# y times t1 in 128x128 tiles, and another order of PE's last products, in an NCHW convolution sequence on one core

## The reference

```python
t1 = p1_w * x                                   # p1_w (1, 128, 64, 1)
t2 = x + t1
t7 = einsum('oc,nchw->nohw', p7_w, relu(x))
t8 = unfold(t7, 1, 5, dilation (1, 3), pad (0, 6))
t9 = x[:, :, None] - t8
t5 = unfold(x, 3, 7, pad (1, 3))                # 21 taps of each channel
t10 = einsum('ngihw,goi->ngohw', t2 in 4 groups, p10_w)
t11 = einsum('nck,nmk->ncm', t1, t5) / sqrt(h * w)
t12 = t9.mean(2)                                # over the 5 taps
t13 = einsum('ncm,nmk->nck', t11, t10) / sqrt(c * 21)
out = maximum(t13, t12)
```

## Time and profile before

| | |
|---|---|
| median of 3 runs | 408.89 us (408.26 to 410.04) |
| profiled execution | 409.05 us, span 407.1 us |
| PE busy | 395.0 us, 97% |
| DVE busy | 333.5 us, 82% |
| ACT busy | 249.5 us, 61% |
| POOL busy | 89.2 us, 22% |
| instructions | 12373, of them PE 5126 matmuls and 5126 loads |
| granted TensorE clock | 1.00 |

### The profile page before, as it was taken

One profiled execution on the slowest core, in us unless ns is written; L12 is line 12 of the kernel. 1 busy time (PEld: TensorE's weight loads), 2 busy tenths in 40 slices (PEclk: granted clock), 3 DMA queues, 4 the chain that ended last, 5 costly groups with the idle time before them and its releaser, 6 DMA issues.

```text
span 407.1 us, 12373 instructions
## 1 busy us (share of the span) xinstructions
PE 395.0 (97%) x5126; PEld 253.8 (62%) x5126; DVE 333.5 (82%) x401; ACT 249.5 (61%) x714; POOL 89.2 (22%) x75
## 2 busy tenths in 40 slices
PE   7999999999999999999999999999999999999985
PEld 2333756668666686666888886444766668444673
DVE  7999958999688887888888887888868889686814
ACT  1336628776677745777277770777727776477980
POOL 0672201232033200332003320033201330033200
PEclk9999999999999999999999999999999999999999
DMA  8973362563766347663575634745455443643105
GB/s 314 405 292 111 105 219 62 183 215 114 293 190 218 112 156 225 197 225 97 174 239 204 190 128 153 255 167 164 163 208 181 162 160 100 208 130 104 53 30 208
DMA packets 24104, 72.40 MB, mean 178 GB/s; under 512 B 2800, under 2 KB 3056, under 8 KB 24048
## 3 DMA queue, kind: packets, MB, share of 16 engines
q1 hardware_dynamic: 24048, 71.61, 51.7%
HBM read 54.82 MB, written 16.78 MB: 176 GB/s over the span
## 4 chain that ended last, share of the span: by engine, by line
PE 85%; issue 5%; POOL 3%; DVE 2%; DMA 1%; ACT 1%; SPq 0%; DVEq 0%; ACTq 0%; POOLq 0%
PE ps_y L681 45%; PE ps_y L693 16%; PE ps_p L693 12%; PE ps_t L693 12%; POOL t1T L219 3%; DMA xw<-x_conv 1%; ACT t L314 0%; DVE v_planes L490 0%; DVE ps_y L509 0%; DVE ps_y L512 0%; DVE v_planes L467 0%; ACT base L259 0%; DVE base L565 0%; DVEq L43 0%; SPq L142 0%
## 5 line engine op out<-in xcount | busy, mean ns | idle before, releaser
L681 PE MATMUL ps_y<-v_planes,u_planes 64*64 64x512 f32 x2048 | 257.9, 590 | 1.1 <-DVE v_planes L469 0.7
L681 PEld LDWEIGHTS ps_y<-v_planes,u_planes 64*64 64x64 f32 x2048 | 127.8, 133 | 91.9 <-issue 42.2
L219 POOL TENSOR_TENSOR t1T<-t1T,p1T_sb 128x512 f32<-128x512 f32 x64 | 83.3, 1329 | 281.1 <-DVE box L540 153.2
L314 ACT ACTIVATE t<-xn,p_plus 128x64 f32<-128x64 f32 x512 | 128.2, 335 | 0.0
L693 PE MATMUL ps_p<-box,p_fifth 64*64 64x512 f32 x464 | 124.7, 590 | 0.7 <-issue 0.7
L693 PE MATMUL ps_t<-t,aT 64*64 64x512 f32 x448 | 119.7, 590 | 0.0
L259 ACT ACTIVATE base<-ps_p 128x512 f32<-128x512 f32 x58 | 34.6, 597 | 84.6 <-PE ps_p L693 84.6
L693 PEld LDWEIGHTS ps_y<-t1T,yT 64*64 64x64 f32 x2048 | 58.8, 133 | 8.0 <-DVE yT L522 3.7
L693 PE MATMUL ps_y<-t1T,yT 64*64 64x128 f32 x2048 | 61.2, 270 | 2.3 <-issue 2.1
L693 PEld LDWEIGHTS ps_p<-box,p_fifth 64*64 64x64 f32 x464 | 40.0, 133 | 20.7 <-issue 9.3
L693 PEld LDWEIGHTS ps_t<-t,aT 64*64 64x64 f32 x448 | 38.9, 133 | 17.7 <-issue 3.7
(11 more groups left out here) (42 smaller groups left out, 117.8 us busy)
## 6 DMA issues: line engine op xcount, KB each, us to landing
xw<-x_conv SPq DMA_DIRECT2D x32, 594.0 KB, 5.5
xn<-x_nat SPq DMA_DIRECT2D x32, 512.0 KB, 4.1
t1T<-x_pix SPq DMA_DIRECT2D x32, 512.0 KB, 6.6
out<-base SPq DMA_DIRECT2D x64, 256.0 KB, 2.5
u_planes<-w_tiles SPq DMA_DIRECT2D x4, 384.0 KB, 5.6
p1T_sb<-p1T SPq DMA_DIRECT2D x1, 128.0 KB, 7.3
p_sb<-p7T SPq DMA_DIRECT2D x1, 64.0 KB, 7.2
p_sb<-p SPq DMA_DIRECT2D x1, 32.0 KB, 7.4
```

The source lines that it names most:

```text
L219: nc.gpsimd.tensor_tensor(part, part, p1T_sb[:, e, :].unsqueeze(1).broadcast_to([P, 4, C]), ALU.mult).then_inc(t1_ready, 1)
L314: last = nc.scalar.activation(t2[:, h, W * r:W * (r + 1)], xn[:, f, at:at + W], ACT.Copy, scale=p1_plus[:, 8 * h + r:8 * h + r + 1])
L681: last = nc.tensor.matmul(dst[TILE * pair:TILE * pair + TILE, :], u_planes[rows, u % GROUPS, weights, TILE * k:TILE * k + TILE], v_planes[ ...
```

## The change

`y_times_t1` uses whole blocks: one product of 128x128 with 128 columns for each of the 32 blocks, all into one bank, `a_bank(n)`. There is no `a_part` any more; ACT alone scales the bank into `aT` (`scale_a`), and DVE's part goes. In the last image `y_times_t1` runs in one piece, and the three p7 pairs come behind it: one directly, one between t13's first two steps, one behind the second. On ACT the scaling moves ahead of `base_half` 5 and `t2_half` 7. `bank_free` no longer waits for `out_ready` at h = 3, and waits for `y_turned` at h = 4.

```diff
-        def a_banks(n):
-            return ps_y[(GROUPS * (n + 1) + 2) % SETS]
+        def a_bank(n):
+            return ps_y[(GROUPS * (n + 1) + 2) % SETS][0]
...
-            def first_part_of_a(n):
+            def scale_a(n):
                 if n < 0:
                     return
                 act.wait_ge(a_done, n + 1)
-                wait(act, aT_ready, n)
-                copy(a_part[:], a_banks(n)[0][:, 0:P], SCALE).then_inc(a_part_ready, 1)
+                wait(act, t13_done, 8 * (n - 1))
+                copy(aT[:, n % 2, :], a_bank(n)[:, 0:P], SCALE).then_inc(aT_ready, 1)
...
             for h in range(4, 7):
                 t2_half(LAST, h)
+            scale_a(LAST)
             base_half(LAST, 5)
             t2_half(LAST, 7)
-            first_part_of_a(LAST)
             base_half(LAST, 6)
             base_half(LAST, 7)
...
-            def second_part_of_a(n):
-                if n < 0:
-                    return
-                dve.wait_ge(a_done, n + 1)
-                dve.wait_ge(a_part_ready, n + 1)
-                wait(dve, t13_done, 8 * (n - 1))
-                nc.vector.scalar_tensor_tensor(out=aT[:, n % 2, :], in0=a_banks(n)[1][:, 0:P], scalar=SCALE,
-                                               in1=a_part[:], op0=ALU.mult, op1=ALU.add).then_inc(aT_ready, 1)
...
-                for t in range(tiles_from, tiles_to):
+                for t in range(2 * BLOCKS):
                     e, j = t // BLOCKS, t % BLOCKS
-                    for half in range(2):
-                        last = half_product(a_banks(n)[half], yT[:, e, j, :], t1T[:, e, j, :], half, t == 0)
-                if tiles_to == 2 * BLOCKS:
-                    last.then_inc(a_done, 1)
+                    last = nc.tensor.matmul(a_bank(n)[:, 0:P], yT[:, e, j, :], t1T[:, e, j, :], start=t == 0,
+                                            stop=t == 2 * BLOCKS - 1)
+                last.then_inc(a_done, 1)
...
-            y_times_t1(LAST, 0, BLOCKS + 6)
+            y_times_t1(LAST)
+
             p7_rows(LAST, 6, 0, True)
             p7_rows(LAST, 5, 1, True).then_inc(item_half, 1)
-            y_times_t1(LAST, BLOCKS + 6, BLOCKS + 12)
-            pe.wait_ge(item_half, done + 6)
-            p7_rows(LAST, 5, 0).then_inc(p7_done, 1)
-            p7_rows(LAST, 7, 1, True).then_inc(item_half, 1)
-            y_times_t1(LAST, BLOCKS + 12, 2 * BLOCKS)
-            pe.wait_ge(item_half, done + 7)
-            p7_rows(LAST, 6, 1).then_inc(p7_done, 1)
-            p7_rows(LAST, 7, 0).then_inc(p7_done, 1)
+
+            def second_step():
+                pe.wait_ge(item_half, done + 6)
+                p7_rows(LAST, 5, 0).then_inc(p7_done, 1)
+                p7_rows(LAST, 7, 1, True).then_inc(item_half, 1)
+
+            def third_step():
+                pe.wait_ge(item_half, done + 8)
+                p7_rows(LAST, 6, 1).then_inc(p7_done, 1)
+                p7_rows(LAST, 7, 0).then_inc(p7_done, 1)
...
             last_first(0)
+            second_step()
             last_first(2)
+            third_step()
             last_second(0)
```

More of the change, by code:

```diff
@@ L70, in conv_seq_kernel @@
         p7_fifth = sb("p7_fifth", [P, P])
-        a_part = sb("a_part", [P, P])
         aT = sb("aT", [P, 2, P])
@@ L116, in conv_seq_kernel @@
         a_done = sem("a_done")
-        a_part_ready = sem("a_part_ready")
         aT_ready = sem("aT_ready")
@@ L353, in _ @@
                     relu(1, 0)
-                    first_part_of_a(0)
+                    scale_a(0)
                     base_half(0, 4)
@@ L374, in _ @@
                     t2_half(1, 3)
-                    first_part_of_a(1)
+                    scale_a(1)
                     t2_half(1, 4)
@@ L394, in _ @@
                     t2_half(n - 1, 4)
-                    first_part_of_a(n - 1)
+                    scale_a(n - 1)
                     base_half(n - 1, 5)
@@ L620, in _ @@
                     box_pairs(0, 3)
-                    second_part_of_a(0)
                     box_fours(0, 3)
@@ L626, in _ @@
                     box_sums(n - 1, 3)
-                    second_part_of_a(n - 1)
                     box_sums(n, 0)
@@ L665, in _ @@
             max_half(LAST - 1, 7)
-            second_part_of_a(LAST)
             for h in range(8):
@@ L744, in zero_three, with y_times_t1 @@
                         last.then_inc(m_done, 1)
[L746 to L752, removed]
-                for t in range(tiles_from, tiles_to):
+            def y_times_t1(n):
+                pe.wait_ge(y_turned, 8 * n + 8)
+                pe.wait_ge(t1_ready, 8 * n + 8)
+                for t in range(2 * BLOCKS):
                     e, j = t // BLOCKS, t % BLOCKS
-                    for half in range(2):
-                        last = half_product(a_banks(n)[half], yT[:, e, j, :], t1T[:, e, j, :], half, t == 0)
-                if tiles_to == 2 * BLOCKS:
-                    last.then_inc(a_done, 1)
+                    last = nc.tensor.matmul(a_bank(n)[:, 0:P], yT[:, e, j, :], t1T[:, e, j, :], start=t == 0,
+                                            stop=t == 2 * BLOCKS - 1)
+                last.then_inc(a_done, 1)
             def p7_rows(n, h, half, first=False):
@@ L821, in slot @@
                 outputs_second(p_a, t_a, item_a)
-                if turned is not None:
+                if turned is not None and turned >= 0:
                     y_times_t1(turned)
@@ L916, in bank_free @@
                     pe.wait_ge(base_ready, 8 * LAST + held + 1)
-                else:
+                elif h == 0:
                     pe.wait_ge(out_ready, 8 * LAST)
+                elif h == 4:
+                    pe.wait_ge(y_turned, 2 * UNITS)
             def last_first(h):
@@ L926, in last_second @@
             def last_second(h):
-                pe.wait_ge(item_half, done + 8 + h // 2)
+                pe.wait_ge(item_half, done + (8 + h // 2 if h else 7))
                 t13_rows(LAST, h, 1).then_inc(t13_done, 1)
```

## The result

The changed kernel takes 406.17 us in the median (405.80 to 407.42, 6 runs) for 408.80 of before on the same chip: ratio 0.9935, 95% interval 0.9914 to 0.9957, that is 2.6 us or 0.65% less. Run once more in another session the ratio was 0.9945 (0.9931 to 0.9959). The forecast was 405.7, with 402.8 to 409.4 around it.

What follows compares the result with a forecast made beforehand. PE was taken as the bound, idle at code stops in bursts and before t13. 409.05 - 3.7 (code) - 1.8 (end) + 0.3 (passes) + 2.0 (changing shape) = 405.85, so a median of 405.7 us, range 402.8 to 409.4.

Steps and rivals of the forecast that it cites:

- What bounds the kernel: Whole span: PE, busy 97%, bounds it, standing still at stops in y times t1 bursts and before t13 at the end.
- Code: Bursts of y times t1: instructions arrive late; fewer, larger products remove the stops, gaining 3.7 us (0 to 4.2).
- the early stop: PE's stop right behind the first burst, 0.67 us at 53.38; removing it was counted as 0.8 us of gain.
- Time of a pass: Each 128x128 product in the bursts: 0.110 to 0.12 us where it was 0.110; 0.3 us taken of 0 to 5.
- the row of the same shape: Full-array loads in the first microseconds: 0.16 us from load to load, taken as 0.08 at 2.4 GHz.
- Rival 3: Burst passes: a full load doesn't hide under 128 columns, deciding from 0.010 us a pass; mostly 411 to 447 us, chance 0.15.
- Changing shape: PE going from tiles to full array and back once an image: 2.0 us cost taken, between nothing and 3.8.
- ACT and DVE: Scaling of A by ACT alone, without DVE's additions: cost and gain nothing, DVE staying near 82%.
- The end: Last image: p7 pairs cover ACT's earlier scaling, so t13 starts without a wait; gain 1.8 us of at most 1.9.
- The slack of 0.5 us: Last image: ACT's last copies end by 397.6, before t13's last first-products want them at 398.1.
- The sum: Whole kernel: 409.05 - 3.7 - 1.8 + 0.3 + 2.0 = 405.85 us profiled, a predicted median of 405.7.
- Rival 1: Tile and full-array switches: changing shape costs its upper end, 407.65 us, or 408.65 with bare loads; chance 0.15.

Runs made afterwards that it cites:

- before_two_bursts: Kernel before, its 64x64 products of y times t1 in two bursts of 16 blocks in six of eight images: 406.56 for 408.91 us, ratio 0.9945.
- late_scale: Changed kernel with ACT's scaling of A behind t2 of half 7 in the last image: 407.82 for 409.06 us, ratio 0.9979.
- p7_ahead: Changed kernel with p7's second and third pair directly behind the first, ahead of t13, in the last image: 406.92 for 409.06 us, ratio 0.9942.

## Why the prediction was right, point by point

**What bounds the kernel**: right. PE is busy for 97 or 98% of the span in every run, and what it saved in the middle came out at the end.

**Code**: the mechanism is right. The same instructions spread out stop less or not at all, and the stops stand at fixed places of the list, 1.2 to 1.6 us behind the end of a transfer; no run changed the fetch by itself. Its size was off: 3.7 us for what measured 5.4. Five stretches of before sum to 244.1 us (48.4, 48.4, 49.1, 49.3, 48.9, from burst to burst); at 48.19 they would be 240.95, so 3.15 went there, not 2.9. The sixth (to the last burst) had 0.7: 45.05 us, and 44.39 in `before_two_bursts`. The first image had 1.6: from tile product to tile product 50.88 became 49.76, although an image is 0.5 dearer. I took the visible idle time only. Breaks too short to show as idle cost 0.2 an image even where I called the burst whole (48.4 for 48.19), and behind the early stop products that should go four abreast went on one and three at a time (53.38, 53.50).

**Time of a pass**: the row of the same shape, halved by the clock, was the wrong bound to take: 0.08 for a load that holds 0.112. The other bound, twice the tile's, was the right one. So the second size was off. Rival 3's mechanism is there, the load no longer hides under 128 columns, but it is a quarter of the 0.010 us from which I let it decide: a pass is 0.0023 us over the tiles' 0.109, 0.15 us an image, 1.2 us for the forecast 0.3.

**Changing shape**: the third size that was off, 0.36 us a pair, 2.9 us in all for the forecast 2.0, between its bounds (0 and 3.8). The Trainium skill's rule, TensorEngine Tiling (Array Packing), Key Properties, that changing the mode drains the engine, is what the timeline agrees with: the first full load starts only 0.09 us after the last tile has streamed, and in the last image no semaphore holds it. What I had priced from the record's length, 0.16 ahead of the load, was too much.

**ACT and DVE**: nothing, as forecast; DVE's share is 82% again.

**The end**: 16.94 us where it was 18.19, with a burst dearer by 0.5: 1.75 for the forecast 1.8. `late_scale` shows that ACT's order gains most of it (1.4), `p7_ahead` that the pairs between t13's steps keep 0.7 of it. The slack of 0.5 us that I gave the last copies on ACT was reckoned too wide: by the prediction's own rows they end at 394.1 + 0.6 + 2.0 + 1.2 = 397.9, 0.2 ahead of 398.1. Nothing hung on it; they ended at 396.52, and PE waited for none.

**The sum** closes in the profiled executions: -5.4 + 2.9 + 1.2 - 1.75 = -3.05, and this profile's first burst began 0.3 us later (44.99 for 44.68): 2.75, for spans of 407.1 and 404.3. The forecast's total, -3.2, came near by luck: the gain from code was too small by 1.7 us, and the two costs, 2.3 for a measured 4.1, by 1.8. The claim "faster" stood on less than it seemed. Rival 1's price as written, 409.05 - 5.5 + 3.8, is 407.35; its 407.65 has the 0.3 of the passes in it too.

## What to carry over

Count instructions for each microsecond, not only in total: a burst of small matmuls can stop for code long after it began, and spreading it over other work cures most of it without an instruction fewer, and here it gained 2.35 us where whole products alone gained 1.05. When a whole product replaces tiles, price three things apart: the load against the columns it streams under, the two edges where the shape changes, and the instructions saved; here the fastest form was the one in between, two tiles of 64 columns. At a kernel's end, look at what the engine that prepares the next operand does just before.

## Not expected of the hardware

A load of 128 columns holds the next one for 0.112 us whether 128 or 64 columns stream, over 64 or 128 rows; one of 64 columns fits under a pass of 0.109. A change of tile shape costs 0.36 us there and back, in columns or in both directions, and 0.31 in rows alone. The first microseconds differ from run to run: the third pass of 512 columns (from 4.89) lasted 0.61 us before and 0.85 after (the pass time that I read as the 1.2 GHz level), with the granted clock reading 1.00 in both. That pass does not set what follows: PE waits behind it for DVE's v_planes in both kernels (0.70 and 0.19 us, until 6.79 and 7.00).
